# First attention of a fused six-layer kernel: score matmuls of one head pair and two tiles in 64 array rows, another order of units, causal masks written by TensorE

## The reference, cut to what matters

```
qkv = x @ Wqkv.T                                   # x: 4 sequences of 1024 tokens, 128 features
q, k, v = heads of 8                               # 16 heads
dots = einsum('bhid,bhjd->bhij', q, k) * dh**-0.5
dots = where(causal_mask, -inf, dots)
attn = softmax(dots, axis=-1)
out = einsum('bhij,bhjd->bhid', attn, v)           # back to 128 features
out @ Wout.T + bout
```

## Time and profile before

| | us |
|---|---|
| median of 3 runs | 1957.57 |
| lowest and highest run | 1955.22, 1958.05 |
| the profiled execution | 1956.27 |
| its span in the profile | 1954.5 |

### The profile page before, as it was taken

How to read it: one execution, slowest core, us unless ns; L and a number is a source line. 1 busy time by engine, 2 the same in 40 slices (tenths; PEclk the granted TensorE clock), 3 DMA queues, 4 the chain that set the end, 5 groups by cost and what they waited for, 6 DMA issues and landing times. The chain is left out here.

```text
span 1954.5 us, 31514 instructions
## 1 busy us (share of the span) xinstructions
PE 1646.7 (84%) x10370; PEld 1169.0 (60%) x10375; DVE 1319.5 (68%) x2575; ACT 934.0 (48%) x1659; POOL 642.4 (33%) x802
## 2 busy tenths in 40 slices
PE   6996784899999999998798778277599999998476
PEld 5665672555555555554666566155368888887354
DVE  6543456888888888782753445699686666662897
ACT  2433332488888888885343333133234444444232
POOL 0785452211111111111088545133243333333132
PEclk9998997899999999999699889699699999999799
DMA  6122322111111111110512232100100000000000
GB/s 238 39 66 72 103 61 70 25 35 32 33 28 28 38 28 39 28 23 13 192 43 77 71 99 62 47 1 0 45 1 2 0 0 0 0 0 2 6 19 19
DMA packets 50298, 82.35 MB, mean 42 GB/s; under 512 B 11236, under 2 KB 35236, under 8 KB 49380
## 3 DMA queue, kind: packets, MB, share of 16 engines
q1 hardware_dynamic: 41092, 62.09, 11.1%
q0 software_dynamic: 9088, 18.76, 2.9%
HBM read 43.19 MB, written 31.22 MB: 38 GB/s over the span
## 5 line engine op out<-in xcount | busy, mean ns | idle before, releaser
L1920 DVE TENSOR_REDUCE z_parts<-z_pM 128x4 f32<-128x512 f32 x576 | 373.3, 686 | 94.6 <-PE z_pM L1658 90.9
L1835 ACT ACTIVATE z_Pr<-z_pE 128x512 f32<-128x512 f32 x576 | 322.5, 596 | 83.8 <-PE z_pE L1682 81.0
L1682 PE MATMUL z_pE<-z_QM,z_QK 128*128 128x512 f32 x576 | 250.4, 437 | 7.3 <-DMA z_QM<-z_Q 4.8
L2027 POOL TENSOR_SCALAR_AFFINE_SELECT z_Pr<-z_Pr 128x512 f32<-128x512 f32 x128 | 81.2, 635 | 480.1 <-ACT z_Pr L1835 480.1
L1658 PE MATMUL z_pM<-z_KM,z_Q 128*128 128x512 f32 x576 | 233.3, 409 | 1.5 <-DVE z_Q L1910 0.9
L1452 POOL TENSOR_TENSOR a_pm<-a_Pn,k_mask 128x512 f32<-128x512 f32 x128 | 132.2, 1057 | 233.5 <-PE a_pT L1291 153.5
L1682 PEld LDWEIGHTS z_pE<-z_QM,z_QK 128*128 128x128 f32 x576 | 107.6, 187 | 158.3 <-ACT z_Pr L1835 91.7
L486 POOL DMA_INDIRECT slot_results<-m_yq,m_xq x156 | 153.5, 984 | 142.9 <-ACT m_yq L690 116.6
L462 POOL DMA_INDIRECT slot_rows<-m_XN,m_dest x128 | 129.3, 1010 | 93.9 <-DVE m_dest L779 58.6
L1695 PE MATMUL z_pO<-z_Pr,z_V 128*9 128x512 f32 (+3 forms) x1536 | 159.3, 488 | 0.1
L834 DVE TENSOR_TENSOR m_h<-m_sg,m_gu 128x512 f32<-128x512 f32 x78 | 53.7, 688 | 111.3 <-ACT m_sg L682 111.3
(11 more groups left out here) (294 smaller groups left out, 3785.5 us busy)
## 6 DMA issues: line engine op xcount, KB each, us to landing
slot_rows<-in_c_pad SPq DMA_DIRECT2D x2, 5070.0 KB, 23.8
m_xq<-slot_rows SPq DMA_DIRECT2D x38, 260.0 KB, 3.0
z_QM<-z_Q SPq DMA_DIRECT2D x128, 64.0 KB, 2.0
z_KM<-z_QK SPq DMA_DIRECT2D x60, 128.0 KB, 2.4
m_raw<-in_gu SPq DMA_DIRECT2D x2, 2048.0 KB, 8.6
m_XN<-slot_results SPq DMA_DIRECT2D x8, 512.0 KB, 6.0
m_raw<-slot_results SPq DMA_DIRECT2D x8, 512.0 KB, 5.5
slot_results<-m_yq,m_xq POOLq DMA_INDIRECT x156, 2.3
```

Of the source, the lines that this page charges most:

```text
L1682: mm(pE[e % 2][:, :].rearrange("p (h c) -> p h c", h=4), QK[G % RING][:, kt * P:(kt + 1) * P], QM[half][:, :, q * P:(q + 1) * P], start=Tr ...
L1835: a.activation(Pr[j % 4][:, :, q * P:(q + 1) * P], pE[e % 2][:, :].rearrange("p (h c) -> p h c", h=4), ACT.Exp, scale=DH0 ** -0.5).then_in ...
L1920: v.tensor_reduce(parts[:, qt, kb, :], pM[n % 3][:, :].rearrange("p (h k) -> p h k", h=4), AX.X, ALU.max).then_inc(maxed, 1)
L2027: g_.affine_select(blk, blk, [[0, 4], [1, P]], ALU.is_ge, 0.0, base=0, channel_multiplier=-1).then_inc(selected, 1)
```

## The change

A unit is still 512 columns, but of two heads (a pair) and two tiles, and it contracts over the pair's 64 partitions alone. Tiles on a diagonal, and the tiles next to one, are paired up in one unit of two matmuls of 256 columns each. Pairs alternate so that exp unit e and max unit e are of different pairs, and the max unit now follows its exp unit directly. The mask is an identity matmul in every round. `fill_mask` and its semaphore are gone. `parts` has 5 slots for a tile in place of 8. An exp unit of two different key tiles is two activations of 256 columns. `select` waits for the last unit that writes its tile. All positions AT_ are others. The diff, cut:

```
-        MU = [(qt, kb) for qt in range(KT) for kb in range(qt + 1)]
-        NM, NM0 = len(MU), 10
+        heads_of = lambda pair: slice(2 * pair, 2 * pair + 2)
+        rows_of = lambda pair: slice(64 * pair, 64 * pair + 64)
+        pair_of_keys = lambda qt, i: (((qt, 2 * i, 2),), PAIR + i)
+        diagonals = lambda qt: (((qt, qt, 1), (qt + 1, qt + 1, 1)), ON_DIAGONAL)
+        singles = lambda qt: (((qt, qt - 1, 1), (qt + 2, qt + 1, 1)), SINGLE)
+        MU0 = [pair_of_keys(2, 0), diagonals(0), pair_of_keys(3, 0), diagonals(2), singles(1)]
+        MU1 = [pair_of_keys(4, 0), pair_of_keys(4, 1), diagonals(4), pair_of_keys(5, 0), pair_of_keys(5, 1), pair_of_keys(6, 0), pair_of_keys(6, 1),
+               diagonals(6), pair_of_keys(6, 2), pair_of_keys(7, 0), pair_of_keys(7, 1), pair_of_keys(7, 2), singles(5)]
+        MU = [(pair, tiles, slot) for tiles, slot in MU0 + MU1 for pair in (1, 0)]
+        NM, NM0 = len(MU), 2 * len(MU0)
+        EU0 = [((0, 0, 0, 2),), ((0, 0, 2, 2),), ((1, 1, 2, 2),), ((1, 1, 1, 1), (3, 3, 3, 1)), ((2, 2, 2, 2),)]
+        EU1 = [((4 + kt, kt, q, 2),) for kt in range(5) for q in (0, 2)] + [((9, 5, 2, 2),), ((9, 5, 1, 1), (11, 7, 3, 1)), ((10, 6, 2, 2),)]
+        EU = [(half, pair, tiles) for half, units in ((0, EU0), (1, EU1)) for tiles in units for pair in (0, 1)]
-        AT_V = (8, 12, 13, 14, 19, 25, 31, 33, 35, 37, 39, 42)
-        AT_TAKE = (14, 6)
-        AT_M1, AT_O1, AT_FIN, AT_K, AT_O0, AT_Q, AT_M0 = 4, 10, (13, 14), (16, 18), 21, (23, 29), 27
-        LATE, AT_MAX = 2, 13
+        AT_V = (9, 11, 13, 15, 20, 22, 27, 31, 35, 36, 40, 41)
+        AT_TAKE = (15, 7)
+        AT_M1, AT_O1, AT_FIN, AT_K, AT_O0, AT_Q, AT_M0 = 2, 11, (14, 15), (17, 18), 24, (25, 33), 29
+        LATE, AT_MAX = 2, 10
...
                 def max_unit(G, n):                                                  (TensorE)
-                    if G and kb == qt:
-                        pe.wait_ge(filled, len(DIAG) * (G - 1) + DIAG.index(n) + 1)
-                    last = mm(pM[n % 3][:, :].rearrange("p (h k) -> p h k", h=4), Q[G % 2][:, qt * P:(qt + 1) * P],
-                              KM[G % 2][:, :, kb * P:(kb + 1) * P], start=(G == 0 or kb < qt), stop=(G > 0 or kb < qt), skip_group_check=True)
-                    if G == 0 and kb == qt:
+                    for i, (qt, kb, nk) in enumerate(tiles):
+                        last = mm(pM[n % 3][:, i * 256:i * 256 + 2 * nk * P].rearrange("p (h k) -> p h k", h=2), Q[G % 2][r, qt * P:(qt + 1) * P],
+                                  KM[G % 2][r, hs, kb * P:(kb + nk) * P], start=(i == 0), stop=(i == len(tiles) - 1), skip_group_check=True)
+                    if slot == ON_DIAGONAL:
                         last = mm(pM[n % 3][:, :], identb[:, :], after_query[:, :], start=False, stop=True, skip_group_check=True)
...
                 def exp_unit(G, e):
-                    mm(pE[e % 2][:, :].rearrange("p (h c) -> p h c", h=4), QK[G % RING][:, kt * P:(kt + 1) * P],
-                       QM[half][:, :, q * P:(q + 1) * P], start=True, stop=True, skip_group_check=True).then_inc(st_ready, 1)
+                    for i, (j, kt, q, nq) in enumerate(tiles):
+                        last = mm(pE[e % 2][:, i * 256:i * 256 + 2 * nq * P].rearrange("p (h c) -> p h c", h=2), QK[G % RING][r, kt * P:(kt + 1) * P],
+                                  QM[half][r, hs, q * P:(q + nq) * P], start=(i == 0), stop=(i == len(tiles) - 1), skip_group_check=True)
+                    last.then_inc(st_ready, 1)
...
                         exp_unit(G, e)                                               (TensorE's main)
+                        if more:
+                            max_unit(G + 1, e)
...
-                        if more:
-                            max_unit(G + 1, e)
...
-                        a.activation(Pr[j % 4][:, :, q * P:(q + 1) * P], pE[e % 2][:, :].rearrange("p (h c) -> p h c", h=4),
-                                     ACT.Exp, scale=DH0 ** -0.5).then_inc(exp_done, 1)
-                        if more and e + 2 in DIAG:
-                            fill_mask(G + 1, e + 2)
-                        if further and e + 2 == NM:
-                            fill_mask(G + 2, 0)
+                        for i, (j, kt, q, nq) in enumerate(tiles):
+                            if e == FIRST_OF[j]:
+                                need(act, pv_done, NJ * G + j - 3)
+                            last = a.activation(Pr[j % 4][:, heads_of(pair), q * P:(q + nq) * P],
+                                                pE[e % 2][:, i * 256:i * 256 + 2 * nq * P].rearrange("p (h c) -> p h c", h=2), ACT.Exp, scale=DH0 ** -0.5)
+                        last.then_inc(exp_done, 1)
...
-                    need(pool, exp_done, NE * G + FIRST_OF[j] + 1)
+                    need(pool, exp_done, NE * G + CROSS[j] + 1)
```

More of the change, by code:

```diff
@@ L1509, in attention0_stage @@
         Pr = [s.sb(f"Pr{u}", [P, 4, 512]) for u in range(4)]
-        parts, m = s.sb("parts", [P, KT, KT, 4]), s.sb("m", [P, KT, 4])
+        ON_DIAGONAL, SINGLE, PAIR, NSLOT = 0, 1, 2, 5
+        parts, m = s.sb("parts", [P, KT, NSLOT, 4]), s.sb("m", [P, KT, 4])
         mw = s.sb("mw", [P, KT, 4, 32], F32R)
@@ L1537, in attention0_stage @@
         k_masked, q_masked = (k0_masked, k1_masked), (q0_masked, q1_masked)
-        sm_ready, maxed, mstep, m_wide, m_turned, m_kept, filled = (
-            s.sem(x) for x in ("sm_ready", "maxed", "mstep", "m_wide", "m_turned", "m_kept", "filled"))
+        sm_ready, maxed, mstep, m_wide, m_turned, m_kept = (
+            s.sem(x) for x in ("sm_ready", "maxed", "mstep", "m_wide", "m_turned", "m_kept"))
         st_ready, exp_done, selected, pv_done = (s.sem(x) for x in ("st_ready", "exp_done", "selected", "pv_done"))
@@ L1555, in attention0_stage @@
-        FIRST_OF = [min(e for e in range(NE) if EU[e][0] == j) for j in range(NJ)]
-        LAST_OF = [max(e for e in range(NE) if EU[e][0] == j) for j in range(NJ)]
-        AT_V = (8, 12, 13, 14, 19, 25, 31, 33, 35, 37, 39, 42)
-        AT_TAKE = (14, 6)
-        AT_M1, AT_O1, AT_FIN, AT_K, AT_O0, AT_Q, AT_M0 = 4, 10, (13, 14), (16, 18), 21, (23, 29), 27
-        LATE, AT_MAX = 2, 13
+        heads_of = lambda pair: slice(2 * pair, 2 * pair + 2)
+        rows_of = lambda pair: slice(64 * pair, 64 * pair + 64)
@@ new lines, in attention0_stage @@
+        NE, NE0 = len(EU), 2 * len(EU0)
+        units_of = lambda j: [e for e in range(NE) if any(tile[0] == j for tile in EU[e][2])]
+        FIRST_OF, LAST_OF = [min(units_of(j)) for j in range(NJ)], [max(units_of(j)) for j in range(NJ)]
+        KEY_TILE = [j if j < 4 else j - 4 for j in range(NJ)]
+        CROSS = [max(e for e in units_of(j) for i, kt, q, nq in EU[e][2] if i == j and q <= kt - 4 * EU[e][0] < q + nq) if j < 4 or j >= 8 else None for j in range(NJ)]
+        AT_V = (9, 11, 13, 15, 20, 22, 27, 31, 35, 36, 40, 41)
@@ L1645, in max_unit @@
                 def max_unit(G, n):
-                    qt, kb = MU[n]
+                    pair, tiles, slot = MU[n]
+                    hs, r = heads_of(pair), rows_of(pair)
                     if G == 0 and n in (0, NM0):
@@ L1674, in exp_unit @@
                 def exp_unit(G, e):
-                    j, half, kt, q = EU[e]
+                    half, pair, tiles = EU[e]
+                    hs, r = heads_of(pair), rows_of(pair)
                     if e in (0, NE0):
@@ L1818, in keep_batch @@
                                  pX[half][:, :].rearrange("p (a n b) -> p a n b", a=1, b=PER), ACT.Copy).then_inc(fin_kept, 1)
-                def fill_mask(G, n):
-                    act.wait_ge(maxed, NM * G + n - 2)
-                    a.activation(pM[n % 3][:, :], after_query[:, :], ACT.Copy).then_inc(filled, 1)
                 def main(G):
                     more, further, first = G + 1 < NG, G + 2 < NG, G % 4 == 0 and G > 0
-                    if G == 0:
-                        fill_mask(1, 0)
                     for e in range(NE):
-                        j, half, kt, q = EU[e]
+                        half, pair, tiles = EU[e]
                         need(act, st_ready, NE * G + e + 1)
-                        if e == FIRST_OF[j]:
-                            need(act, pv_done, NJ * G + j - 3)
-                        a.activation(Pr[j % 4][:, :, q * P:(q + 1) * P], pE[e % 2][:, :].rearrange("p (h c) -> p h c", h=4),
-                                     ACT.Exp, scale=DH0 ** -0.5).then_inc(exp_done, 1)
-                        if more and e + 2 in DIAG:
-                            fill_mask(G + 1, e + 2)
-                        if further and e + 2 == NM:
-                            fill_mask(G + 2, 0)
+                        for i, (j, kt, q, nq) in enumerate(tiles):
[4 more added lines that the diff above has]
+                        last.then_inc(exp_done, 1)
                         if e == AT_M1:
@@ L1919, in max_unit @@
                         need(dve, mstep, 2 * G - 1 if n == 0 else 2 * G)
```

(6 more changed lines are left out.)

3 lines of the change are left out of this document (2 added, 1 removed).

## The result

The changed kernel takes **1945.66 us** (median of 5 runs, 1944.61 to 1953.29), against 1958.05 (5 runs, 1955.22 to 1958.88) beside it: a ratio of **0.9951**, 95% interval 0.9929 to 0.9972. It is faster, by 12 us where 30 were forecast, and inside the stated range. The profiled execution took 1945.66 us.

The account below looks back on a forecast made before the run. TensorE was taken to bound each round; -1.6 us over 15 rounds, 2 us in the lead-in and 3 for odd waits gave -29 from 1956.3, with 1.3 added for the median: 1928 us, range 1882 to 1968.

Parts of the forecast that it names:

- Term 1: Score matmuls of each round: exp and max units in different row halves stream at once, -8.3 us a round.
- Rival B: At every pair the second matmul starts late; at 0.30 us a pair about 1969 us, slower; chance 0.14.
- Term 3: TensorE's new switches between 64-row and 128-row work in a round, with drains and open weight loads: +4.6 us.
- Rival A: Change of array shape nearly free, at most 0.1 us a stop; round 29.0 us, whole 1882 us; chance 0.28.
- Term 4: Second weight load of a pair between stops: loads side by side, taken as 0 but for +0.3 us a round.
- Term 2: Eight mask matmuls a round moved onto TensorE: +1.8 us.
- The sum: All TensorE terms of a round together: -1.6 us, giving a round of 32.3 us.
- The waits: Per round, TensorE's 0.25 us wait for QM mostly goes; ScalarE waits up to 1.2 us for VectorE's split, taken as 0.2.
- Rival C: Nothing moves: errors cancel or a ScalarE stop at e = 18 takes up to 1.2 us a round; 1957 us; chance 0.06.
- the lead-in: Before round 0: the 0.50 clock stays as before, pairs side by side save 2 us, bounds 0 and 5.6.
- the last round: Round without max units: two more shape changes, four split units, overlapping exp units; net 0, bounds -1 and +2 us.
- The other sign: Outside the changed layer: another layer moving by over 2 us would show the forecast wrong.

Follow-up runs that it names:

- e7: Changed kernel with the pair order of max units swapped, so exp unit and max unit e share one row half: 1985.8 us.
- e6: Changed kernel with dummy matmuls filling TensorE's lead-in stop and round 0's max units over all 128 rows: 1925.8 us.
- e1: Changed kernel with every score matmul over all 128 rows, new order and units kept: 1979.8 us.
- e8: Changed kernel with VectorE taking row maxima over only the first half of each tile's keys: 1947.1 us.
- e2: Changed kernel with only round 0's max units, which run in the lead-in, over all 128 rows: 1934.5 us.
- e5: Changed kernel, 64 rows everywhere, with 28 dummy 128-row matmuls where TensorE waits for VectorE's cast in the lead-in: 1932.4 us.
- e9: e6 with the last round's exp units over all 128 rows too: 1924.1 us.
- e3: e2 with the last round's exp units over all 128 rows too: 1930.9 us.
- e4: Changed kernel without the eight mask matmuls of the row maxima in rounds 1 to 15: 1931.8 us.
- e10: e9 with ScalarE instead of TensorE writing the masks of rounds 1 to 15: 1944.0 us.
- e11: e9 with the turned maximum moved from e = 29 to 28 and the first key projection from 17 to 16: 1931.1 us.

## Why the prediction was right in its rounds and wrong in its size

**Term 1** (-8.3, halves side by side): right. Starts lie together, and e7 shows that the halves make it. The figure of the Trainium skill that I weighed against it ("TensorE: Matmul & The Clock Gate", "Measured speedup vs the span model": 3.07x for four row tiles), by which I had a pair at 0.30 us, does not apply to a pair here: after a stop the next pair starts after 0.34, of which 0.11 is the weights, so 0.23. The same section's few nanoseconds between starts do agree. Rival B is out.

**Term 3** (+4.6, changes of shape): right, 0.10 us of drain each way and 0.11 for the weights, as values had shown. Around a projection the stop costs 0.41 in all (533.39 to 534.72 is 1.33, less 4 x 0.23), where I had 0.42; around a mask 0.30 (522.06 to 522.81 is 0.75, less 2 x 0.23), where I had 0.36. The Trainium skill's rule ("TensorEngine Tiling (Array Packing)", "Key Properties") that a change of mode drains holds for rows as for columns; the trace gives it 0.09 to 0.10 us. Rival A is out, as half rows are no cheap change. **Term 4** (0 for second loads): right, two loads at 520.32. **Term 2** (+1.8, masks): right. Where masks and units have one shape (e6's lead-in), a unit and a mask together take 0.47 us (masks at 364.56 and 365.03), 2 x 0.23.

**The sum** was a round of 32.3, and it is 31.9. e1, which undoes terms 1, 3 and 4, differs by 3.54 where they sum to 3.4. The waits came as named, with other sizes: ScalarE waits 0.7 us a round for VectorE's split (I had up to 1.2), but the wait for QM did not go: it is 1.1 us a round by the weight loads' record, which already had 0.7 in the kernel before, where I had taken 0.25 from the matmuls' record. VectorE stays busier than 26.9 us (386.86 of the 440 us from 410 on, so 28.0 a round): its row maxima still take 0.66 us each (25.6 us for 39 in the stretch above), not the 0.616 of the earlier trace rows. It is near the bound, but e8 shows that it isn't the bound. Rival C's wait is real and too small.

**The step that failed is the lead-in**, "I take 2" saved, between 0 and 5.6, and with it the last round, "0, bounds -1 and +2". Measured: +12.2 and +4.5, and +2.4 in round 0, which I had with the 15 equal rounds at -1.6. Two things in that step were wrong.

The first is the clock. I read the 0.50 in the earlier trace rows and took for granted that it would end where it had ended. Its state depends on what TensorE does, and the change alters that. e1 and e2 take 14.5 and 11.6 us off the lead-in by the rows alone, e5 13.0 by the stop alone.

The second is the sign of the saving at any clock. I wrote that the values' projections "change shape and remain". In the kernel before they change nothing, as projections and max units both have 128 rows; the changes of shape there are new, and term 3, which counts them in a round, was not applied to the lead-in. With the clock at 1.00 on both sides (e5 and e6) half rows cost 4.3 us where I had 2 saved. In the last round it is the clock: full rows there take 2.6 us off (37.0 in e6, 34.4 in e9) and end 0.5 below the kernel before.

Without most of this loss the whole comes near the forecast: e2, e3 and e5, which remove it in three ways, have ratios of 0.9878, 0.9871 and 0.9849, 24 to 30 us below the kernel before, and 1928 us would have been 0.985. The other sign that I had named, another layer that moves by over 2 us, did appear, as the layer begins 4.5 us earlier. It says nothing here, since traces of unchanged code differ by more than that.

The direction was right and the size, 12 us for 30, was less than half. The range held the time only because it was wide for other reasons: no case in it was about the clock.

## What to carry to other kernels

Row halves side by side took two matmuls in the time of one here, less 0.1 us of drain each way and an open weight load at every matmul of another shape between them; count those stops before the change is made, in the stretches at the ends too. Where short matmuls of 128 rows are mixed in, as in this lead-in, the stops cost more than the halves save. Before cutting the rows of a matmul, look where the clock is below 1.00 or TensorE stands still for several us: there give it full-row work (zero rows leave the result as it is, and a matmul of 512 columns takes 0.23 us with 64 or 128 rows; what is given up is the second half beside it) or dummies, and keep half rows for the dense part. When a steady loop gains what the sum says and the whole does not, cut both traces at the same events, and read PEclk for each piece.

## What the runs showed of the hardware that was not expected

- After the stop TensorE's clock stayed at 0.50 for 47 to 50 us with TensorE's busy time at 4 to 5 of every 5 us, when the score matmuls used 64 rows (the changed kernel, e4, e7, e8). With 128 rows and the same order it was at 1.00 again 8 to 13 us after the stop (e1, e2, e3), though KM and QM are zero in the added rows. The Trainium skill ("TensorE: Matmul & The Clock Gate", "What's actually happening") says that the clock follows how busy TensorE has been. The busy time of the profile does not tell the two apart here: in the changed kernel and in e2 it was 5.00 of 5 in each of the three stretches from 353 to 368 us.
- In the dense middle rounds half rows held 1.00 throughout, but for three rounds of e10. In the last round, with the max units gone, all seven kernels with half rows there (the changed one, e2, e4 to e8) had stretches of 5 us below 1.00, and took 35.6 to 40.2 us: 35.6 with some 3 us at 0.50, 37.0 with 7, 39.4 to 40.2 with 14 (worked out from PEclk). The five with full rows (e1, e3, e9 to e11) were at 1.00 until the last exp unit and took 34.4 to 34.9. By these rows a microsecond at 0.50 costs about 0.4 us there. Why the dense rounds hold the clock with half rows and the last round does not was not tried.
- Weight loads into two row halves run at the same time (both at 520.32), where two loads of 128 rows are 0.11 us apart.
